# Four matmul banks, longer rings and second expert weights addressed by a register, in the sparse mixture of a two-layer gated network

## The chip, the cores and the metric

One core of one Trainium2 chip runs the whole program. The metric is device time in microseconds (us) of one execution. Engines are TensorE (PE, its weight loads PEld), VectorE (DVE), ScalarE (ACT), GpSimd (POOL) and SyncE (SP, here a queue of DMA issues).

## The reference

Inputs are x (128 x 64 x 128, which is 8192 tokens of 128 numbers) and a context (128 x 64 x 96). Everything is float32.

```python
x = x + tanh(g_xattn[0]) * cross_attention_16_heads(layernorm(x), ctx)      # layer 0
x = x + tanh(g_ffn[0])   * mixture_of_6(layernorm(x))    # all 6 experts, 64 hidden, weights of the best 2
x = x + tanh(g_xattn[1]) * cross_attention_1_head(layernorm(x), ctx)        # layer 1
x = x + tanh(g_ffn[1])   * mixture_of_8(layernorm(x))    # the change is here
# mixture_of_8: logits = x @ Wg; the two largest, softmax over the two; for each expert e
#   h = silu(x @ W1[e]) * (x @ W2[e])        128 -> 256
#   out += (h @ W3[e]) * weight[e]           256 -> 128
```

## The kernel before

The first phase (up to about 320 us) is the 16-head attention, in 64 tiles of 128 tokens. The second phase (function mixtures_and_attention) does the first mixture, the second attention and the routing of the last mixture in 16 groups of 512 tokens, as a software pipeline over STEPS, and then the last mixture as a sparse one. The queues of the engines are written out by hand: each engine has its own unrolled list of calls, and semaphores are the only link between them.

The sparse mixture works on sorted rows. For each token the two chosen experts give two rows, which POOL scatters with indirect DMAs (L1105, 8 for each group) into a table in HBM sorted by expert. The table is worked off in DTILES = 142 tiles of 128 rows (71 for each half of the tokens), each of one expert; a plan made on DVE gives the first row and the expert of every tile. Step t of `sparse(t)`, one for each engine, does:

- SP: the load of the rows of tile t (L1063, ring of 7 buffers).
- PE: the hidden matmuls of tile m = t - HIDDEN (L1741: four logical 128x128x128 float32 matmuls, W1 and W2 of the expert, recorded as 8), the transpose of tile t (L1751, one record), and the output matmuls of tile w = t - OUT (L1760: two logical, recorded as 4). Then it raises `ends_mm`. The hidden matmuls raise `hidden_mm`.
- ACT: silu of tile t - HIDDEN out of the bank (L1510), and a copy of W1 and W2 of tile t's expert, 128x512, from the resident weights into a ring of 3 (L1517).
- DVE: waits for `ends_mm` of t + 1, which is PE's step t; copies the transposed tile to SBUF (L1285), keeps its token numbers and weights (L1286), multiplies silu by the second half of the bank for tile t - HIDDEN (L1290, raises `h_ready`), scales the output of tile t - OUT (L1301, raises `share_ready`), and copies W3 of tile t's expert, 128x256, into a ring of 8 (L1307). Every fourth step it first loads four expert numbers into registers (`four_tiles`, L902).
- POOL: one indirect DMA (L1113) for each tile, which scatters its 128 scaled rows to their tokens' places in a table of contributions. `keep_shares(b)` does four tiles.

With HIDDEN = 2 and OUT = 4 the waits between the steps are these. PE's hidden matmuls of step t wait for `h_ready` m - 1, the product of tile t - 4, which DVE makes in its step t - 2: there are two hidden banks, `uv[m % 2]`. PE's output matmuls of step t wait for the product of tile t - 4 and the share of tile t - 6, both from DVE's step t - 2. DVE's step t waits for PE's step t. ACT's silu waits for `h_ready` m - 1 too (two silu buffers).

The first 17 steps are woven into what is left of groups 14 and 15 of the dense part: in POOL's queue `keep_shares(0)` (tiles 0 to 3) stands before the scatter of group 14, and `keep_shares(1)` and `keep_shares(2)` stand before the scatter of group 15. From step 108 on DVE also adds contributions of the first half to X (L1322). After the last tile the contributions of the second half are loaded (eight loads of 512 KB), added (L1328, L1330) and stored.

## Time and profile before

| | |
|---|---|
| median of 3 runs | 926.17 us (923.63 to 931.97) |
| profiled execution, its own time | 930.39 us |
| span of the profiled execution | 928.6 us, 1.8 us less than its time |
| mean granted TensorE clock | 0.933 |
| PE busy | 793.4 us, 85% |
| DVE, ACT, POOL busy | 720.4, 571.9 and 466.9 us |

Busy time is the time in which an engine had an instruction running. Starts of PE's records are measured and their ends are modelled; starts and ends of DVE and ACT are measured. The number in brackets at the end of a line of the timeline is how long the engine had been idle and who ended that.

### The profile page before, as it was taken

The page shows a single profiled execution, that of the slowest core. Times are in us where ns is not written, and L with a number is a line of the kernel's source. Part 1 is how long each engine was busy: PE and PEld are TensorE (multiplying, and loading weights), DVE is VectorE, ACT ScalarE, POOL GpSimd, SP SyncE. Part 2 cuts the span into 40 slices and gives each one's busy share as a digit, 9 for nine tenths or more (in the row PEclk, how much of TensorE's full clock was granted, in tenths as well). Part 3 has the DMA queues.
Part 4 walks back from the last instruction along what each step waited for, and adds up shares of the span by engine and source line. Part 5 has one row for each costly group of instructions (what it writes and reads, how often), then busy time and mean ns, then how long its engine had stood idle before and what let it go on. Part 6 is the DMA issues. An engine that isn't in the chain of part 4 may idle for free. (4 is left out here: it accounts for less than half of the span.)

```text
span 928.6 us, 26325 instructions
## 1 busy us (share of the span) xinstructions
PE 793.4 (85%) x8408; PEld 610.8 (66%) x8408; DVE 720.4 (78%) x3041; ACT 571.9 (62%) x1209; POOL 466.9 (50%) x504
## 2 busy tenths in 40 slices
PE   4999999999999599999998898865678888888870
PEld 2566666666666356677775676765577887888860
DVE  3989899889898769899999988644465666668864
ACT  3777777777776456887887766443334555555530
POOL 3653454445444011376676765646555554555550
PEclk9999999999999879989999989877779999999995
DMA  9001001000100200011111111311122322245628
GB/s 242 30 23 41 20 20 37 22 20 20 39 1 2 59 1 10 13 50 45 46 45 39 53 44 35 88 49 58 58 67 73 96 79 69 78 125 163 178 81 277
DMA packets 62211, 57.95 MB, mean 62 GB/s; under 512 B 10320, under 2 KB 52099, under 8 KB 62115
## 3 DMA queue, kind: packets, MB, share of 16 engines
q1 hardware_dynamic: 44547, 34.25, 13.2%
q0 software_dynamic: 8640, 17.84, 5.7%
q10 hardware_dynamic: 8928, 4.70, 1.8%
q8 instruction: 45, 0.74, 0.3%
q14 instruction: 51, 0.42, 0.2%
HBM read 32.74 MB, written 24.02 MB: 61 GB/s over the span
## 5 line engine op out<-in xcount | busy, mean ns | idle before, releaser
L1113 POOL DMA_INDIRECT contributions<-v_heads,d_token x142 | 136.6, 962 | 120.4 <-DVE v_heads L1301 76.2
L1741 PE MATMUL bc_bank<-d_xT,d_w 128*128 128x128 f32 x1136 | 161.9, 288 | 39.7 <-DVE b_hidden L1290 17.1
L1741 PEld LDWEIGHTS bc_bank<-d_xT,d_w 128*128 128x128 f32 x1136 | 145.7, 201 | 46.8 <-DVE d_xT L1285 35.1
L1105 POOL DMA_INDIRECT sorted_rows<-r_send,r_slots x128 | 126.8, 990 | 50.2 <-issue 34.6
L1510 ACT ACTIVATE b_hidden<-bc_bank 128x256 f32<-128x256 f32 x142 | 54.4, 383 | 154.4 <-PE bc_bank L1741 121.1
L1285 DVE COPY d_xT<-bc_bank 128x128 f32<-128x128 f32 x142 | 40.8, 287 | 94.3 <-PE bc_bank L1760 66.3
L432 POOL TENSOR_SCALAR a_k_heads<-a_kT,first 128x512 f32<-128x512 f32 x60 | 93.2, 1570 | 0.8 <-ACT a_kT L483 0.8
L1517 ACT COPY d_w<-w 128x512 f32 x142 | 86.9, 612 | 2.2
L507 ACT ACTIVATE a_probs<-a_scores 128x1024 f32<-128x1024 f32 x64 | 65.6, 1025 | 29.4 <-PE a_scores L607 29.3
L350 DVE TENSOR_REDUCE a_neg_max<-a_scores 128x16 f32<-128x1024 f32 x64 | 78.1, 1220 | 6.8 <-PE a_scores L597 5.3
L514 ACT COPY a_probsT<-a_probsT_bank 128x512 f32<-128x512 f32 x128 | 74.7, 584 | 11.7 <-PE a_probsT_bank L624 11.1
L624 PE MATMUL a_probsT_bank<-first,a_probs 128*128 128x128 f32 x512 | 79.7, 278 | 2.2 <-ACT a_probsT L514 0.3
L347 DVE TENSOR_REDUCE a_denom<-a_probs 128x16 f32<-128x1024 f32 x64 | 77.3, 1208 | 1.7 <-issue 1.3
L597 PE MATMUL a_scores<-a_k_heads,a_qT 32*64 32x256 f32 x1024 | 70.8, 391 | 2.8 <-issue 2.7
L624 PEld LDWEIGHTS a_probsT_bank<-first,a_probs 128*128 128x128 f32 x512 | 57.6, 141 | 12.5 <-issue 5.8
L423 POOL TENSOR_TENSOR X<-X,out_bias 128x512 f32 (+1 forms) x16 | 20.3, 1270 | 87.5 <-ACT a_xn L470 84.8
L1751 PE MATMUL bc_bank<-first,d_rows 128*128 128x128 f32 x142 | 40.6, 286 | 20.7 <-DVE d_xT L1285 14.7
L1586 PE MATMUL bc_bank<-b_xnT,w 128*128 128x512 f32 x96 | 52.9, 666 | 0.9 <-DVE b_weighted L1156 0.9
L1637 PE MATMUL bc_bank<-w,b_weighted 128*128 128x128 f32 x384 | 49.7, 289 | 0.0
L1301 DVE TENSOR_SCALAR v_heads<-bc_bank,d_ends 128x128 f32<-128x128 f32 x142 | 48.8, 344 | 0.5 <-issue 0.5
L1637 PEld LDWEIGHTS bc_bank<-w,b_weighted 128*128 128x128 f32 x384 | 46.9, 202 | 1.8 <-issue 0.4
L1760 PE MATMUL bc_bank<-w_in,b_hidden 128*128 128x128 f32 x288 | 46.8, 288 | 0.5 <-issue 0.5
(215 smaller groups left out, 1884.8 us busy)
## 6 DMA issues: line engine op xcount, KB each, us to landing
d_rows<-sorted_rows SPq DMA_DIRECT2D x142, 65.0 KB
X<-in_x SPq DMA_DIRECT2D x16, 256.0 KB, 3.0
b_hidden<-contributions SPq DMA_DIRECT2D x8, 512.0 KB
b_weighted<-contributions SPq DMA_DIRECT2D x8, 512.0 KB
out_x<-X ACTq DMA_DIRECT2D x16, 256.0 KB
ctxT<-in_ctx_T SPq DMA_DIRECT2D x16, 192.0 KB, 2.9
c_ctxT<-in_ctx_T SPq DMA_DIRECT2D x16, 192.0 KB
contributions<-v_heads,d_token POOLq DMA_INDIRECT x142
```

The source lines that it names most:

```text
L347: dve.reduce_sum(denom[:], probs[u % 2][:].rearrange("p (h k) -> p h k", k=S), AX_X).then_inc(sum_done, 1)
L350: dve.tensor_reduce(neg_max[:], scores[u % 2][:].rearrange("p a (h k) -> p (a h) k", k=S), AX_X, ALU.max, negate=True).then_inc(max_done, 1)
L432: last = pool.tensor_scalar(keys_of_head(par, j), kT[:], c.head_of_group[:, j:j + 1], None, ALU.mult)
L507: act.activation(probs[(u + 1) % 2][:], scores[(u + 1) % 2][:].rearrange("p a n -> p (a n)"), ACT.Exp, scale=SCALE0).then_inc(exp_done, 1)
L514: act.copy(probsT[u % 2][:, half * HU // 2:(half + 1) * HU // 2, :].rearrange("p u q -> p (u q)"), probsT_bank[:]).then_inc(pT_ev, 1)
L597: last = pe.matmul(scores[u % 2][S * b:S * b + S, s, bass.ts(h, 4 * S)], qT[par][rows_in, h, tile, :], k_heads[par][rows_in, tile, h].rear ...
L624: last = pe.transpose(probsT_bank[:, bass.ts(k, P)], probs[u % 2][:, bass.ts(half * HU // 2 + k, P)], c.ident[:])
L1105: pool.indirect_dma_start(dispatch.rows, bass.IndirectOffsetOnAxis(ap=slots[n % 2][:, k, j:j + 1], axis=0), send[n % 2][k][:, j, :], None) ...
L1113: pool.indirect_dma_start(dispatch.contributions, bass.IndirectOffsetOnAxis(ap=token[:, t % KEEP:t % KEEP + 1], axis=0), shares[t % KEEP], ...
L1517: act.copy(w12[t % 3][:], c.w12[:, bass.ds(experts[t % 4], 1)].rearrange("d a i h -> d (a i h)")).then_inc(w12_ready, 1)
L1637: last = pe.matmul(y[:, bass.ts(j, P)], weighted[n % 2][:, k, bass.ts(j, P)], c.w2_0[:, k, :], start=(k == 0), stop=(k == C0 - 1))
L1741: last = pe.matmul(uv[m % 2][:, bass.ts(i, P)], w12[m % 3][:, bass.ts(i, P)], xT[m % 4][:], start=True, stop=True)
```

## The change

Four edits, all in the sparse mixture.

1. The hidden matmuls use four banks instead of two from tile 20 (FOUR) on: banks 0 and 1 and the two halves of `pair`. Up to tile 19 they use banks 0 and 1 in turn, because `pair` is still used by groups 14 and 15. PE's wait before them becomes `h_ready` m - 3 from tile 24 on and stays m - 1 up to tile 21; tiles 22 and 23 wait for the last uses of `pair`.
2. The steps lie further apart: HIDDEN is 3 instead of 2, the product on DVE has a distance of its own, GATED = 4, and OUT is 6 instead of 4. So in step t PE does the hidden matmuls of tile t - 3 and the output matmuls of tile t - 6, ACT the silu of tile t - 3, and DVE the product of tile t - 4 and the share of tile t - 6. The whole takes 148 steps of PE and DVE instead of 146.
3. The ring of silu buffers has 4 instead of 2, in space that was there; ACT waits for `h_ready` m - 3.
4. The copy of W3 on DVE is gone, with its semaphore and its register loads. PE reads W3 where it lies, `c.w3[:, bass.ds(experts[w % 4], 1), k]`, as the moving operand at an address from a register. For this PE loads four expert numbers into its registers every fourth step.

```diff
--- before.py
+++ after.py
@@ -975,16 +975,15 @@
     STEPS = range(-1, G + 3)
 
     KH = HID1 // P
-    HIDDEN, OUT = 2, 4
+    HIDDEN, GATED, OUT, FOUR = 3, 4, 6, 20
     KEEP = 32
     ROWS = 7
     rows = [sb(f"d_rows{i}", [P, ROW], F32) for i in range(ROWS)]
     xT = [sb(f"d_xT{i}", [D, P], F32) for i in range(4)]
     w12 = [sb(f"d_w12_{i}", [D, 2 * HID1], F32) for i in range(3)]
-    w3 = [c.w3_in[:].rearrange("p e k d -> p e (k d)")[:, i] for i in range(8)]
     tails = [b[:, C0 - 1, i * KH * P:(i + 1) * KH * P] for b in hidden + weighted for i in range(2)]
-    silu = tails[0:2]
-    d_hidden = [b.rearrange("p (k n) -> p k n", k=KH) for b in tails[2:6]]
+    silu = tails[0:4]
+    d_hidden = [b.rearrange("p (k n) -> p k n", k=KH) for b in tails[4:8]]
     shares = [c.v_heads[i // (KEEP // 2)][:].rearrange("p g u s -> p (g u s)")[:, i % (KEEP // 2) * D:i % (KEEP // 2) * D + D]
               for i in range(KEEP)]
     token = sb("d_token", [P, KEEP], U32)
@@ -992,13 +991,16 @@
     both = [b[:].rearrange("p c n -> p (c n)")[:, 0:GT * 2 * D].rearrange("p (t k d) -> p t k d", t=GT, k=2)
             for b in hidden + weighted]
 
-    uv, y_bank = bank[0:2], (bank[5], bank[2])
+    y_bank = bank[5], bank[2]
+
+    def uv(m):
+        return (bank[0][:], bank[1][:], pair[:, 0], pair[:, 1])[m % 2 if m < FOUR else m % 4]
 
     def tr_bank(t):
         return bank[4] if t > 16 and t % 2 else bank[3]
 
     d_loaded = [sem(f"d_loaded{i}") for i in range(ROWS)]
-    d_xT_ready, row_read, w12_ready, w3_ready = (sem(f"d_{n}") for n in ("xT_ready", "row_read", "w12_ready", "w3_ready"))
+    d_xT_ready, row_read, w12_ready = (sem(f"d_{n}") for n in ("xT_ready", "row_read", "w12_ready"))
     hidden_mm, ends_mm, silu_done, h_ready, share_ready = (sem(f"d_{n}") for n in ("hidden_mm", "ends_mm", "silu_done", "h_ready", "share"))
     kept = [sem(f"d_kept{i}") for i in range(8)]
     pair_loaded = [sem(f"d_pair_loaded{i}") for i in range(4)]
@@ -1273,8 +1275,6 @@
                     wait_alone(dve, dot_step, 2 * n + 2)
                     top.choose(dve, n)
 
-            experts = [None] * 4
-
             def sparse(t):
 
 
@@ -1284,11 +1284,11 @@
                         dve.wait_ge(hidden_mm, t - 3)
                     dve.tensor_copy(xT[t % 4][:], tr_bank(t)[:, 0:P]).then_inc(d_xT_ready, 1)
                     dve.tensor_copy(ends[:, t % KEEP, :], rows[t % ROWS][:, D:ROW]).then_inc(row_read, 1)
-                m = t - HIDDEN
+                m = t - GATED
                 if 0 <= m < DTILES:
                     dve.wait_ge(silu_done, m + 1)
-                    dve.tensor_tensor(d_hidden[m % 4].rearrange("p k n -> p (k n)"), silu[m % 2],
-                                      uv[m % 2][:, KH * P:2 * KH * P], ALU.mult).then_inc(h_ready, 1)
+                    dve.tensor_tensor(d_hidden[m % 4].rearrange("p k n -> p (k n)"), silu[m % 4],
+                                      uv(m)[:, KH * P:2 * KH * P], ALU.mult).then_inc(h_ready, 1)
                 w = t - OUT
                 if w >= 0:
                     dve.wait_ge(row_read, w + 1)
@@ -1300,11 +1300,6 @@
                         dve.tensor_copy(token[:, here], ends[:, here, 0])
                     dve.tensor_scalar(shares[w % KEEP], y_bank[w % 2][:, 0:D], ends[:, w % KEEP, 1:2], None,
                                       ALU.mult).then_inc(share_ready, 1)
-                if t < DTILES:
-                    if t % 4 == 0:
-                        dve.wait_ge(dispatch.planned, 1 if t + 4 <= HALF_TILES else 2)
-                        experts[:] = dispatch.four_tiles(mybir.EngineType.DVE, dispatch.tile_expert, t, E1 - 1)
-                    dve.tensor_copy(w3[t % 8], c.w3[:, bass.ds(experts[t % 4], 1)].rearrange("p a b d -> p (a b d)")).then_inc(w3_ready, 1)
                 g, q = (t - ADDS_AT) // 4, (t - ADDS_AT) % 4
                 if 0 <= g < GH:
                     add_piece(g, q // 2, q % 2)
@@ -1505,9 +1500,9 @@
                 m = t - HIDDEN
                 if m >= 0:
                     act.wait_ge(hidden_mm, m + 1)
-                    if m >= 2:
-                        act.wait_ge(h_ready, m - 1)
-                    act.activation(silu[m % 2], uv[m % 2][:, 0:KH * P], ACT.Silu).then_inc(silu_done, 1)
+                    if m >= 4:
+                        act.wait_ge(h_ready, m - 3)
+                    act.activation(silu[m % 4], uv(m)[:, 0:KH * P], ACT.Silu).then_inc(silu_done, 1)
                 if t < DTILES:
                     if t % 4 == 0:
                         act.wait_ge(dispatch.planned, 1 if t + 4 <= HALF_TILES else 2)
@@ -1726,6 +1721,8 @@
                         last = pe.transpose(pT_bank[:, bass.ts(j, P)], probs[:, j, :], c.ident[:])
                     last.then_inc(pT_mm, 1)
 
+            experts = [None] * 4
+
             def sparse(t):
 
 
@@ -1733,12 +1730,16 @@
                 if 0 <= m < DTILES:
                     pe.wait_ge(d_xT_ready, m + 1)
                     pe.wait_ge(w12_ready, m + 1)
-                    if m >= 2:
-                        pe.wait_ge(h_ready, m - 1)
+                    if m < 2:
+                        pe.wait_ge(k_ready if m == 0 else weighted_ready[0], G)
+                    elif m == FOUR + 2:
+                        pe.wait_ge(xrT_ready, G)
+                    elif m == FOUR + 3:
+                        pe.wait_ge(x1_updated, G)
                     else:
-                        pe.wait_ge(k_ready if m == 0 else weighted_ready[0], G)
+                        pe.wait_ge(h_ready, m - 1 if m < FOUR + 2 else m - 3)
                     for i in range(2 * KH):
-                        last = pe.matmul(uv[m % 2][:, bass.ts(i, P)], w12[m % 3][:, bass.ts(i, P)], xT[m % 4][:], start=True, stop=True)
+                        last = pe.matmul(uv(m)[:, bass.ts(i, P)], w12[m % 3][:, bass.ts(i, P)], xT[m % 4][:], start=True, stop=True)
                     last.then_inc(hidden_mm, 1)
                 if t < DTILES:
                     pe.wait_ge(d_loaded[t % ROWS], 16 * (t // ROWS) + 16)
@@ -1751,13 +1752,16 @@
                     last = pe.transpose(tr_bank(t)[:, 0:P], rows[t % ROWS][:, 0:D], c.ident[:])
                 if w >= 0:
                     pe.wait_ge(h_ready, w + 1)
-                    pe.wait_ge(w3_ready, w + 1)
+                    if w % 4 == 0:
+                        pe.wait_ge(dispatch.planned, 1 if w + 4 <= HALF_TILES else 2)
+                        experts[:] = dispatch.four_tiles(mybir.EngineType.PE, dispatch.tile_expert, w, E1 - 1)
                     if w >= 2:
                         pe.wait_ge(share_ready, w - 1)
                     else:
                         pe.wait_ge(q_ready if w == 0 else chosen_ready, G - w)
                     for k in range(KH):
-                        last = pe.matmul(y_bank[w % 2][:, 0:D], d_hidden[w % 4][:, k, :], w3[w % 8][:, bass.ts(k, D)],
+                        last = pe.matmul(y_bank[w % 2][:, 0:D], d_hidden[w % 4][:, k, :],
+                                         c.w3[:, bass.ds(experts[w % 4], 1), k].rearrange("p a d -> p (a d)"),
                                          start=(k == 0), stop=(k == KH - 1))
                 last.then_inc(ends_mm, 1)
```

## Rows read from the trace of the kernel before

**Rows 1.** Windows, whole stretches; columns are named in its first line.

```profile
core 0: us, PE busy (x) PEld busy (x) DVE busy (x) ACT busy (x) POOL busy (x), PEclk, DMA share, GB/s
692.70:837.60 144.90, 123.89 (x1055) 119.37 (x1054) 93.47 (x431) 73.61 (x162) 77.46 (x81) 1.00 0.30 86
837.60:898.80 61.20, 52.22 (x434) 50.65 (x433) 48.88 (x207) 30.37 (x67) 32.30 (x34) 0.97 0.50 149
898.80:928.60 29.80, 3.53 (x30) 3.18 (x28) 14.04 (x28) 0.84 (x3) 5.75 (x6) 0.63 0.70 236
```

**Rows 2.** Line L1285 from 692.6 us on: DVE's steps.

```profile
L1285 DVE COPY d_xT<-bc_bank x115: 270/291/293, 692.7 to 898.8; 128x128 f32<-128x128 f32 x115
...
  PE bc_bank L1760: 59.6, 55
```

**Rows 3.** Timeline 703 to 710 us, PE and DVE: start, us, engine, line.

```profile
700.81 0.61 PE L1760 MATMUL bc_bank<-w_in,b_hidden 128*128 128x128 f32 x4
...
703.41 0.29 DVE L1285 COPY d_xT<-bc_bank 128x128 f32<-128x128 f32 x1 [2.25 <-PE bc_bank L1760]
...
704.25 1.13 PE L1741 MATMUL bc_bank<-d_xT,d_w 128*128 128x128 f32 x8 [1.38 <-DVE b_weighted L1290]
...
705.32 0.61 PE L1760 MATMUL bc_bank<-w_in,b_weighted 128*128 128x128 f32 x4
...
705.77 1.06 PE L1741 MATMUL bc_bank<-d_xT,d_w 128*128 128x128 f32 x8
705.97 0.29 DVE L1285 COPY d_xT<-bc_bank 128x128 f32<-128x128 f32 x1 [0.28 <-PE bc_bank L1760]
...
706.58 0.35 DVE L1301 TENSOR_SCALAR v_heads<-bc_bank,d_ends 128x128 f32<-128x128 f32 x1
...
706.77 0.61 PE L1760 MATMUL bc_bank<-w_in,b_weighted 128*128 128x128 f32 x4
...
707.22 1.06 PE L1741 MATMUL bc_bank<-d_xT,d_w 128*128 128x128 f32 x8
...
708.74 0.29 DVE L1285 COPY d_xT<-bc_bank 128x128 f32<-128x128 f32 x1 [1.62 <-PE bc_bank L1760]
...
709.02 0.41 DVE L1290 TENSOR_TENSOR b_hidden<-b_hidden,bc_bank 128x256 f32<-128x256 f32 x1
...
709.58 1.13 PE L1741 MATMUL bc_bank<-d_xT,d_w 128*128 128x128 f32 x8 [0.75 <-DVE b_hidden L1290]
```

**Rows 4.** Groups by line, 692 to 838 us.

```profile
L1113 POOL DMA_INDIRECT contributions<-v_heads,d_token x83 | 79.5, 957 | 68.8 <-DVE v_heads L1301 45.0 <-issue 23.8
...
L1510 ACT ACTIVATE b_hidden<-bc_bank 128x256 f32<-128x256 f32 x82 | 31.4, 383 | 71.0 <-PE bc_bank L1741 66.4 <-issue 3.2 <-DVE b_hidden L1290 1.0
...
L1307 DVE COPY w_in<-w 128x256 f32 x82 | 23.7, 289 | 0.0
```

**Rows 5.** Register work of the sequencers, lines L902, L563 and L591.

```profile
L902 ACTq TENSOR_LOAD <-plan_tile_expert x36: 304/309/517, 606.8 to 896.5; - x36
L902 DVEq TENSOR_LOAD <-plan_tile_expert x36: 339/344/598, 608.0 to 897.6; - x36
...
L563 PEldq FUSED_REGOPS  x12: 78/83/91, 55.0 to 257.5; - x12
...
L591 PEldq FUSED_REGOPS  x6: 51/51/52, 54.2 to 238.3; - x6
```

**Rows 6.** Line L1285 up to 692.6 us: the first 27 steps.

```profile
L1285 DVE COPY d_xT<-bc_bank x27: 269/291/292, 608.0 to 691.5; 128x128 f32<-128x128 f32 x27
...
  remote: 20.2, 4
```

**Rows 7.** Timeline 628 to 681 us, POOL.

```profile
636.45 1.00 POOL L1105 DMA_INDIRECT sorted_rows<-r_send,r_slots  x1 [0.30 <-issue]
...
650.58 0.96 POOL L1113 DMA_INDIRECT contributions<-v_heads,d_token  x1 [0.30 <-issue]
655.86 0.96 POOL L1113 DMA_INDIRECT contributions<-v_heads,d_token  x1 [4.32 <-DVE v_heads L1301]
```

## The prediction

> **What bounds the kernel now.** I read the windows first, because the change touches one stage only, and in them the two long stretches from 692.7 to 898.8 us: the sparse mixture by itself. Granted clock is 1.00 and 0.97, and no engine is full: PE is busy for 123.9 of 144.9 us, DVE for 93.5, POOL for 77.5 [rows 1]. The last 29.8 us are DMA (236 GB/s) and adds, and the change doesn't touch them [rows 1]. Then I took the pace from the line that runs once a step, the copy of the transposed tile: 115 steps, first at 692.7 and last at 898.8 us, so 206.1 / 114 = 1.808 us a step [rows 2]. In the first of the two stretches it is 1055 PE records / 13 a step = 81 steps, 1.785 us.
>
> PE alone could go faster. Where it isn't held, one step starts 1.45 us after the last (705.77, 707.22) [rows 3]. So 114 x (1.808 - 1.45) = 41 us of the stage is PE waiting for its partners, and this is all that a better pipeline can give. DVE is busy for 93.5 / 81 = 1.15 us a step [rows 1], and POOL's scatter takes 0.96 plus 0.30 idle = 1.26 us [rows 4, 7]; neither is the bound, but POOL has only 0.19 us of room if PE goes at its own pace.
>
> The timeline shows the loop. PE's step that starts at 704.25 has its last matmul done at 705.32 + 0.61 = 705.93; DVE starts its step at 705.97, 0.04 later. For the next step PE's record ends at 706.77 + 0.61 = 707.38, and DVE starts only at 708.74, though it had been idle for 1.62 us: 1.36 late. Two steps earlier it was 700.81 + 0.61 = 701.42 to 703.41, 1.99 late [rows 3]. DVE waits for nothing but PE's semaphore there; 55 such waits cost it 59.6 us in the stage [rows 2]. So the result of a step becomes visible late when PE has gone on to the next without a break, and at once when PE has just been idle. Ends of PE records are modelled, so I call the difference L, the lateness, and take it as it is; what makes it I can't tell.
>
> **The loop before.** PE's hidden matmuls of step t wait for DVE's step t - 2, which waits for the end of PE's step t - 2. Around two steps: L, then from DVE's copy to the end of its product 709.43 - 708.74 = 0.69, to PE's start 709.58 - 709.43 = 0.15, and PE's whole step 705.93 - 704.25 = 1.68 us [rows 3]. That is 2.52 + L = 2 x 1.79, so L = 1.06 on average, between the 0.04 and 1.99 seen.
>
> **The change, part by part.**
>
> *Four banks and HIDDEN = 3, from tile 24 on.* The hidden matmuls of step t need the product of tile t - 7, from DVE's step t - 3, which is always there. They leave the loop. The silu too has a whole step of slack before DVE's product, and its ring of four doesn't wait; ACT waits for PE alone today (66.4 of its 71.0 idle us in the stretch [rows 4]), so this costs nothing.
>
> *The output matmuls stay in the loop.* The product of tile t - 6 and the share of tile t - 8 both come from DVE's step t - 2, as before. The new loop: L, then DVE's copy to the end of the share, 706.93 - 705.97 = 0.96, then 0.15, then the four output records, 0.61 [rows 3]. That is 1.72 + L for two steps. With L = 1.06 a step is 1.39 us, less than PE's 1.45, with 1.36 it is 1.54 and with 1.99 it is 1.86. What is late next, when the stall before the hidden matmuls goes, is a shorter stall before the output matmuls.
>
> *PE's register work.* The trace has no matmul with a register address and no register load on PE. Nearest rows: four expert numbers load in 0.31 us on ACT and 0.34 on DVE, so 0.08 a tile; an address computation on PE's own sequencer, in the loop of the first phase, is 51 to 83 ns [rows 5]. With one to four such for a tile it is 0.05 to 0.33, together 0.13 to 0.41 us a tile, or nothing if PE's sequencer does it while the array is busy. A gain is excluded, since nothing on PE is removed but a wait for a semaphore that DVE raised steps earlier. I put 0.2 us on the loop of two steps, since the computation stands behind the wait for the share: (1.92 + L) / 2. With L = 1.2, between its average and the 1.36 that a continuing PE shows, 1.56; I take 1.55 us a step.
>
> The register load can be weighed against the Trainium skill. The rows have 0.31 to 0.34 us for a load of four. The Trainium skill (DMA: Bandwidth & Descriptors, latency and other measured facts) gives `tensor_load` a floor of about 600 ns, amortised by unrolling four times; the trace disagrees. By the page it would be 0.15 a tile, 0.07 more, and fully exposed 114 x 0.07 = 8 us more than by the rows.
>
> *The W3 copy leaves DVE.* 82 copies, 23.7 us, mean 289 ns in the first stretch, none of which ended an idle time before it [rows 4]. It stands behind the share, so nothing in the loop waits for it, and DVE isn't full: I cost it at nothing there. Between 837.6 and 898.8 us DVE also adds pieces and is busy for 48.9 of 61.2 us [rows 1]; over 34 steps that is 1.44 us each, near 1.55, and without the copy's 0.29 it is 1.15, so the 1.55 holds in this stretch too.
>
> *Steady stage:* 114 x (1.808 - 1.55) = 29 us less.
>
> *The first 25 steps get worse.* Up to tile 21 the hidden matmuls of tile m wait for the product of tile m - 2, and with GATED = 4 and HIDDEN = 3 that is DVE's step t - 1, not t - 2. PE can't start a step before DVE has answered the last one: 0.04 + 0.69 + 0.15 + 1.68 = 2.56 us a step, with L at its smallest since PE has just been idle. Before, 11 of these steps took less than that, between 1.3 and 2.0 us, in all 11 us less (by the starts of the 27 copies [rows 6]). But this stretch is held by other things: of 84 us for 27 steps, 20.2 are four long waits of DVE for PE [rows 6], and from 636.45 to 651.5 us POOL issues without a break, then idles for 4.32 us until tile 8's share comes [rows 7]. POOL's first three `keep_shares` need DVE's steps 9, 13 and 17 instead of 7, 11 and 15, and the scatter of group 15 stands behind the third. Two steps are 3 to 5 us. Part of both falls into POOL's 4.3 us of idle time, or shortens the long waits. I take 8 us of 0 to 16.
>
> *The end:* two more steps to drain, with only four PE records each; under 2 us, and part of POOL's last scatters hide it. Nothing.
>
> **Sum.** 930.4 - 29 + 8 = 909 us on the profiled execution, whose own time is 4.2 us above the median of the runs shown. On the median: 926.2 - 21 = 905 us.
>
> **The rivals.**
>
> *PE at its own pace.* If L doesn't grow and the register work is hidden, the loop is 1.39 and PE's 1.45 us decides, say 1.47: 114 x 0.338 = 38.5 us, and with nothing lost at the start 888 us. For it: L averages 1.06. Against: only 0.19 us of room for POOL. Chance 0.15.
>
> *L grows.* PE now goes on without a break, and L was largest just when it did. With L = 1.85 the step is 1.79 to 1.89 and all that is left is the worse start: 926 + 8 = 934 us; with L = 1.5 it is 1.71, 11 us gained, 923. One form of this: PE's results come late while POOL issues its scatters back to back. All four long waits, of 20.2 us in all [rows 6], fall into or around POOL's unbroken stretches [rows 7], and at a faster pace POOL has less idle time. The Trainium skill (SBUF — State Buffer, who interferes with whom) says that PE never waits for another engine's port and that DMA never contends with a compute engine. It would exclude this form; the waits stand in the trace all the same. Chance of 917 to 935 us: 0.19.
>
> *Slower: the register work isn't hidden on PE.* The engine with the least room gets instructions that DVE had room for. If a matmul with a register address adds c to PE's own 1.45 us, the stage gives nothing back from the point where 114 x (1.808 - 1.45 - c) equals the 8 us of the start, c = 0.29 us a tile; the upper bound of the rows is 0.41. With c = 0.41 a step is 1.86: 114 x 0.05 = 6 us more, plus 8, is 940 us. For it: PE's sequencer has 26 records and three waits to issue in 1.45 us. Against: the registers of four tiles are loaded once, and right after a wait of 1.38 us PE's eight records take the same 1.13 us as after others [rows 3], so the sequencer keeps up with the array. Chance 0.16, with all that ends over 935.
>
> *The change doesn't do what it says:* if four banks weren't reached in time (tile 23 waits for group 15's last add to X), the wait would lie before 692.7 us; in DVE's queue that add stands before its step 6, and PE's wait at its step 26, so it can't be. Less than 0.01.
>
> **How the numbers follow.** Forecast, 893 to 917 us: 0.50. PE's pace, below 893: 0.15. L grows: 0.19. Slower: 0.16. A measurement of this kernel tells about 1% (9 us) from no change. So faster by over 1% (under 917) has 0.50 + 0.15 = 0.65, within 1% 0.19, slower 0.16. The range leaves out the deep end of the first rival (under 889) and most of the last (over 935).
>
> **What the profile after would show.** The copy L1285 at steps of 1.55 us from step 27 on, in place of groups of three with a gap. PE's idle time, if any, before the output matmuls and with DVE's share as releaser, none before the hidden ones. The distance from PE's modelled end to DVE's start at 1.2 us on average: this is the number that would make me wrong, and if it is above 1.7 the gain is gone. Four output records more than 0.61 us apart in all, or register rows on PE in front of them that end an idle time, would be the last rival. In the first 25 steps a steady idle time of PE of about 1.1 us a step, with DVE's product as releaser. POOL's idle before its scatters down from 68.8 us in 146.

## The result, and the profile after

The changed kernel takes 943.2 us (median of four runs, 932.1 to 948.4), the kernel before 929.1 us (four runs, three of them those of its own section). The ratio leaves out the run of 948.4 us, which counts as slow, and is 1.0126, 95% interval 1.007 to 1.0182. The change makes the kernel slower by 1.3%; the forecast was 905 us. Its profiled execution has a span of 938.6 us, 10.0 more than before.

DVE's copy of the transposed tile, line L1285, comes once a step and splits the 10 us. Its occurrences, the first 24 and the other 118, in the changed kernel:

```profile
L1285 DVE COPY d_xT<-bc_bank x24: 283/292/293, 607.3 to 699.4; 128x128 f32<-128x128 f32 x24
...
  PE bc_bank L1763: 24.9, 11
  remote: 18.4, 4
...
L1285 DVE COPY d_xT<-bc_bank x118: 267/291/293, 703.4 to 905.4; 128x128 f32<-128x128 f32 x118
...
  PE bc_bank L1763: 71.0, 63
...
  PE bc_bank L1752: 9.2, 9
```

And the same two stretches of the kernel before:

```profile
L1285 DVE COPY d_xT<-bc_bank x24: 272/291/292, 608.0 to 686.3; 128x128 f32<-128x128 f32 x24
...
L1285 DVE COPY d_xT<-bc_bank x118: 269/291/293, 688.0 to 898.8; 128x128 f32<-128x128 f32 x118
```

- Steps 0 to 24: 703.4 - 607.3 = 96.1 us, before 688.0 - 608.0 = 80.0. **16 us lost** (the first step came 0.7 us sooner).
- Steps 24 to 141: 202.0 us or 1.726 a step, before 210.8 or 1.802. **9 us gained.**
- From the last copy to the end: 938.6 - 905.4 = 33.2 us, before 29.8. **3.4 us lost.**

A second pair of traces, before_again and change_again in the table below, gives 16.4 lost, 2.7 gained and 3.0 lost. The loss at the start and at the end comes again; the gain between them is 3 to 9 us.

The windows of the changed kernel in these three stretches (columns as in [rows 1]):

```profile
607.00:703.40 96.40, 58.71 (x325) 54.02 (x325) 30.61 (x161) 29.55 (x65) 42.30 (x48) 0.68 0.16 46
703.40:905.40 202.00, 184.82 (x1524) 174.77 (x1524) 123.08 (x537) 102.91 (x235) 111.10 (x116) 0.99 0.38 108
905.40:938.60 33.20, 6.07 (x48) 5.32 (x46) 15.45 (x32) 1.45 (x4) 7.65 (x8) 0.62 0.63 213
```

In the second, PE is now busy for 185 of 202 us: 1.58 us a step, though 13 records 0.111 us apart are 1.45. So of the 32 us that the 117 steps take beyond 117 x 1.45, 15 lie where PE counts as busy and its records are further apart, and 17 are idle. PE's waits in this stretch (us, times, longest) account for all of the idle time but 0.4 us, and none of them stands before the hidden matmuls (L1742), where they all stood before:

```profile
PE bc_bank L1752 <- DVE d_xT L1285: 9.2, 9, 2.7
...
PE bc_bank L1763 <- DVE v_heads L1301: 7.6, 16, 0.6
```

In the same 117 steps of the kernel before PE is idle for 30.0 us, 28.9 of them waiting for DVE's product. The first stretch of the changed kernel has a granted clock of 0.68.

**The start.** PE's timeline from 692 to 703 us, where the clock is at its lower level (granted 0.50, 1.2 GHz, over 691.4 to 703.4 us):

```profile
696.28 2.05 PE L1742 MATMUL bc_bank<-d_xT,d_w 128*128 128x128 f32 x8 [0.87 <-DVE b_weighted L1290]
698.12 0.42 PE L1752 MATMUL bc_bank<-first,d_rows 128*128 128x128 f32 x1
698.33 1.06 PE L1763 MATMUL bc_bank<-w,b_weighted 128*128 x4
700.26 2.04 PE L1742 MATMUL bc_bank<-d_xT,d_w 128*128 128x128 f32 x8 [0.87 <-DVE b_weighted L1290]
```

Each step waits for DVE's product of the step before it: 700.26 - 696.28 = 3.98 us a step. Seven of the 24 steps go so (654.2 to 670.1 and 691.5 to 703.4 us); at 670.1 to 677.8 us, where the granted clock is 0.95, three steps take 2.56 us each, the figure of the prediction. Among the first 24 steps of the kernel before, by the starts of their copies, there is no such series.

**The lateness.** By this I mean the time from the modelled end of the last output matmul of a step on PE to the start of DVE's copy for that step. DVE from 746 to 752 us, and below it PE. The step that ends at 746.63 + 0.61 = 747.24 us on PE is answered at 749.98, 2.74 us late; then DVE does its next two steps at once. PE had gone on at its own pace until 749.59 and then stood still, waiting for DVE:

```profile
746.83 0.34 DVE L1301 TENSOR_SCALAR v_heads<-bc_bank,d_ends 128x128 f32<-128x128 f32 x1
749.98 0.29 DVE L1285 COPY d_xT<-bc_bank 128x128 f32<-128x128 f32 x1 [2.80 <-PE bc_bank L1763]
...
750.91 0.28 DVE L1285 COPY d_xT<-bc_bank 128x128 f32<-128x128 f32 x1
...
751.99 0.29 DVE L1285 COPY d_xT<-bc_bank 128x128 f32<-128x128 f32 x1
```

```profile
746.63 0.61 PE L1763 MATMUL bc_bank<-w,b_weighted 128*128 x4
...
748.53 1.06 PE L1742 MATMUL bc_bank<-d_xT,d_w 128*128 128x128 f32 x8
750.41 0.30 PE L1752 MATMUL bc_bank<-first,d_rows 128*128 128x128 f32 x1 [0.83 <-DVE d_xT L1285]
```

Averaged over steps 24 to 141 it is 1.15 us in the changed kernel and 0.87 in the kernel before.

### The profile page after: what moved, and what is told of

Read it like the earlier page. It is cut to its first block and busy times, and to the rows that moved or that the text cites. A ratio compares the mean times of both kernels' runs of the same rounds, so it can differ in the third digit from the quotient of the medians.

```text
span 938.6 us, 26325 instructions
## 1 busy us (share of the span) xinstructions
PE 806.9 (86%) x8408; PEld 618.1 (66%) x8408; DVE 691.3 (74%) x2899; ACT 568.9 (61%) x1209; POOL 466.1 (50%) x504
## 5 line engine op out<-in xcount | busy, mean ns | idle before, releaser
L1285 DVE COPY d_xT<-bc_bank 128x128 f32<-128x128 f32 x142 | 41.0, 289 | 135.0 <-PE bc_bank L1763 96.0
L1742 PE MATMUL bc_bank<-d_xT,d_w 128*128 128x128 f32 x656 | 100.3, 302 | 35.5 <-DVE b_weighted L1290 28.9
L1742 PEld LDWEIGHTS bc_bank<-d_xT,d_w 128*128 128x128 f32 x656 | 90.7, 214 | 39.4 <-DVE d_xT L1285 37.3
L1763 PE MATMUL bc_bank<-w,b_weighted 128*128 x568 | 96.5, 295 | 9.3 <-DVE v_heads L1301 9.2
L1763 PEld LDWEIGHTS bc_bank<-w,b_weighted 128*128 128x128 f32 x568 | 78.9, 201 | 17.4 <-issue 14.3
L1505 ACT ACTIVATE b_hidden<-bc_bank 128x256 f32<-128x256 f32 x82 | 31.5, 385 | 96.2 <-PE bc_bank L1742 50.7
L1505 ACT ACTIVATE b_hidden<-bc_pair 128x256 f32<-128x256 f32 x60 | 23.0, 384 | 70.5 <-PE bc_bank L1742 40.4
L1742 PE MATMUL bc_pair<-d_xT,d_w 128*128 128x128 f32 x480 | 64.3, 277 | 0.0
L1742 PEld LDWEIGHTS bc_pair<-d_xT,d_w 128*128 128x128 f32 x480 | 59.3, 194 | 0.0
```

What stands on the lines that cost most here:

```text
L1742: last = pe.matmul(uv(m)[:, bass.ts(i, P)], w12[m % 3][:, bass.ts(i, P)], xT[m % 4][:], start=True, stop=True)
L1763: last = pe.matmul(y_bank[w % 2][:, 0:D], d_hidden[w % 4][:, k, :], c.w3[:, bass.ds(experts[w % 4], 1), k].rearrange("p a d -> p (a d)"), ...
```

## The experiments

Each group of runs had a chip of its own, with its own runs of the kernel before, so every ratio is to that chip's. The kernel before took 856 to 947 us on them, a wider spread than any effect of the change, and that became part of the question. All of it in one table (steps from the starts of the copy of the transposed tile, as above; "per step" is over steps 24 to 141, "tail" from the last copy to the end; times in us). Runs with "plain_shares" in their name and one_load_hidden compute something else than the reference; they are there for their times only.

```
run                     before on    ratio, 95% interval       steps 0-24  per step  tail
                        that chip
(kernel before, shown above)                                     80.0      1.802     29.8
(changed kernel)         929.1    1.0126  1.007  to 1.0182        96.1      1.726     33.2
w3_alone                 947.2    1.0067  1.0036 to 1.0098        79.7      1.939     32.4
banks_alone              947.2    1.0124  1.009  to 1.0157        98.2      1.857     34.0
equal_gates              947.2    0.9854  0.9808 to 0.9901        79.1      1.731     32.9
old_gates_banks          947.2    0.9861  0.9805 to 0.9916        77.9      1.756     30.7
before_again             927.6    (one run, 928.9 us)             77.0      1.782     30.0
plain_shares             927.6    0.9565  0.9454 to 0.9675        75.4      1.450     28.9
one_load_hidden          927.6    0.9944  0.9927 to 0.996         85.0      1.663     34.5
before_plain_shares      858.3    0.9946  0.9912 to 0.9979        47.6      1.451     26.6
equal_gates_w3_copy      858.3    1.0009  0.998  to 1.0038        48.3      1.445     32.8
change_again             928.4    1.0091  1.0058 to 1.0124        93.4      1.759     33.0
equal_gates_again        928.4    0.996   0.9916 to 1.0004        77.8      1.764     30.9
w3_copy_again            928.4    1.0072  1.0038 to 1.0106        77.6      1.811     31.5
four_steps_deep          857.1    1.0012  0.9984 to 1.004         47.3      1.448     34.0
four_steps_deep_again    855.9    1.0013  0.9984 to 1.0043        47.9      1.448     33.8
four_steps_deep_third    945.9    0.9874  0.9813 to 0.9935        76.9      1.734     32.7
```

### Parts and distances

**w3_alone**: the kernel before, with

```
-  w3_ready, the ring w3[0..7] and DVE's copy (L1303 to L1307 of the kernel before)
-  pe.wait_ge(w3_ready, w + 1)
+  if w % 4 == 0: pe waits for the plan and loads four expert numbers
-  ... w3[w % 8][:, bass.ts(k, D)]
+  ... c.w3[:, bass.ds(experts[w % 4], 1), k]
```

> The kernel before with one part of the change: the second expert weights read in place by TensorE through a register address, DVE's W3 copy gone; two banks, rings and distances as before. Theory R (the register work costs PE time where PE has none to give): 138 tiles at 0.05 to 0.15 us make it 7 to 20 us slower than the kernel before, and the copy of the transposed tile goes at 1.85 to 1.95 us a step in place of 1.80. Theory N (it is hidden, and DVE's copy hid too): within 4 us of the kernel before, 1.79 to 1.82 us a step.

**banks_alone**: the changed kernel with that edit undone.

> The changed kernel with the second expert weights copied by DVE again, as before: four banks, HIDDEN 3, GATED 4, OUT 6 stay. Theory R: the register work was what ate the gain, so this one is 7 to 20 us faster than the changed kernel and at 1.60 to 1.68 us a step. Theory N: within 4 us of the changed kernel, 12 us slower than the kernel before, at 1.71 to 1.74 us a step, and the first 24 steps are as long as in the changed kernel.

**equal_gates**:

```
-    HIDDEN, GATED, OUT, FOUR = 3, 4, 6, 20
+    HIDDEN, GATED, OUT, FOUR = 3, 3, 5, 20
```

> The changed kernel with GATED 3 in place of 4 and OUT 5 in place of 6, HIDDEN 3 as it is: DVE's product of a tile no longer comes one step after the hidden matmuls' step, so the two-bank stretch needs DVE's step t-2 again and not t-1. Theory S (the chain PE, DVE, PE with one step between, in the first 24 steps, costs the 16 us): step 24 is reached 12 to 16 us sooner than in the changed kernel, the later steps stay at 1.72 to 1.75 us, and the whole is 12 to 16 us faster than the changed kernel, 0 to 5 us faster than the kernel before. Rival (the start is held by POOL's late shares and the row loads, not by the chain): step 24 comes less than 6 us sooner.

**old_gates_banks**: banks_alone with `HIDDEN, GATED, OUT, FOUR = 2, 2, 4, 20`.

> The kernel before with the four banks alone: HIDDEN 2, GATED 2, OUT 4, W3 copied by DVE, but banks and silu ring of four from tile 20 on. Theory S: the first 24 steps as in the kernel before within 3 us. The later steps tell whether the larger distances bring anything: if the hidden matmuls' wait for their bank was the loop, 1.72 to 1.75 us a step, 6 to 9 us faster than the kernel before; if the loop goes through the output matmuls, which still need DVE's step t-2, and the silu of the step that has just ended, 1.77 to 1.80 us a step and no difference.

Theory S holds: with GATED equal to HIDDEN the first 24 steps take 79.1 us (77.8 in the repeat) where the changed kernel has 96.1 (93.4) and banks_alone 98.2, and the whole is faster than the changed kernel by 12 us on one chip (0.996 against 1.0091 of 928 us) and 25 us by the ratios of two (0.9854 against 1.0126). The rival, that the start is held by the shares that come later on POOL, isn't needed. Here OUT went from 6 to 5 together with GATED, but four_steps_deep_third (below) has OUT 6 again with GATED 3, is the same kernel up to step 24 otherwise, and takes 76.9 us on a chip with late results. And the series of 3.98 us a step is gone. In the first 24 steps of equal_gates DVE's waits for PE by name have shrunk, 24.9 to 7.5 us; those labelled "remote", explained below, have not (18.4 to 25.6):

```profile
L1285 DVE COPY d_xT<-bc_bank x24: 272/290/292, 609.6 to 687.2; 128x128 f32<-128x128 f32 x24
...
  remote: 25.6, 4
  PE bc_bank L1763: 7.5, 9
```

old_gates_banks is as good as equal_gates: 1.756 us a step, 13 us faster than the kernel before, more than the 6 to 9 expected of it. So what gains on this chip is the four banks; the greater distance of the hidden matmuls, with W3 in place, adds nothing to the whole (0.9854 beside 0.9861). The distance alone, with all else equal, was not run on one chip.

Theory R fell. W3 in place cost 0.7% with two banks (6 us, just under the 7 expected), and its 1.939 us a step lies in the theory's range, though the kernel before has no trace on that chip to compare with. But in that run PE waits before its hidden matmuls alone, 46 us for DVE's product, and never before the output matmuls, where the register work stands. Undone in the changed kernel it gave nothing back by the ratios on two chips (1.0124 beside 1.0126), at 1.857 us a step, a pace that neither theory had. And at equal gates, side by side on one chip, in place was better by 1.1% (equal_gates_again, w3_copy_again, below). No price of register work on PE comes out; its four-number loads take 0.33 us each. Where nothing is late, the pace is the same with W3 in place (1.450 in plain_shares, 1.448 in four_steps_deep) and copied (1.451 in before_plain_shares, 1.445 in equal_gates_w3_copy).

### What makes PE's results late

**before_again** is the kernel before.

> The kernel before once more, for a profile on the same chip as the next ones: 1.79 to 1.90 us a step after step 24, 80 us for the first 24 steps. No theory differs here; it is the measure for the other three.

It has 1.782 us a step and 77.0 us for the first 24 steps, both a little under that.

**pe_alone_and_scatters** holds only this on PE, with no wait (in short):

```
for t in range(30):
    4 x pe.matmul(bank[t % 2][:, 128 i : 128 i + 128], w_i, xT)   -> increments hid
    pe.transpose(...)
    2 x pe.matmul(bank[3 + t % 2], ...)                           -> increments end
POOL: 39 x pool.indirect_dma_start(table, slots[:, i], src)       (stretches b, d, f)
SP:   39 x sp.dma_start(table rows, src)                          (stretch c)
```

> A kernel of its own that computes nothing of the reference (its output is x): six stretches of 30 steps, each with PE's work of one step and no wait on PE, four hidden matmuls on four loads, one transpose, two output matmuls. a: PE alone; b: with POOL's indirect scatters back to back; c: with the same bytes as plain transfers; d: the hidden matmuls as one load with 512 columns, with scatters; e: with copies on DVE and ACT; f: e with scatters. Small copies on DVE and ACT after each step tell when its result is really there. Theory T1 (PE's true pace for load and matmul in turn is slower than its records of 1.45 us a step): DVE's copies come 1.65 to 1.75 us apart in a, b, c, e and f alike, and under 1.45 in d. Theory T2 (POOL's descriptor work holds PE's results back): 1.45 in a, c and e, and in b and f over 1.65 or copies late by 1 to 3 us in groups. Theory T3 (the transfers themselves hold them back): c is like b. Theory T4 (none of these; the lateness is of the loop's own copies): 1.45 everywhere, and no lateness.

Alone, PE keeps 1.45 us a step and DVE's small copy comes 1.45 us after the last; with 39 plain transfers (c) too. Windows of a, b and c:

```profile
24.00:65.00 41.00, 41.00 (x366) 41.00 (x366) 4.75 (x28) 5.36 (x28) 0.00 (x0) 1.00 0.01 1
72.00:119.00 47.00, 17.29 (x105) 14.93 (x104) 1.41 (x6) 0.96 (x5) 35.73 (x38) 0.65 0.15 53
158.00:199.00 41.00, 41.00 (x370) 41.00 (x370) 4.74 (x28) 5.39 (x28) 0.00 (x0) 1.00 0.22 64
```

105 PE records in 47 us beside POOL's scatters, 370 in 41 us beside the plain transfers, which move more (64 against 53 GB/s). T2 holds, T1 and T3 fall. The other stretches agree: with scatters DVE's copies fall behind in the same way when the hidden matmuls are one load with 512 columns (d, up to 18 us apart) and with copies on DVE and ACT (f, 20 us), and with those copies and no scatters (e) they come 1.45 us apart. DVE in stretch b: the results come at distances that double, to 25 us:

```profile
73.70 0.34 DVE L38 COPY tiny<-xT 128x2 f32<-128x2 f32 x1 [1.28 <-PE bank L31]
75.45 0.17 DVE L38 COPY tiny<-xT 128x2 f32<-128x2 f32 x1 [1.42 <-PE bank L31]
79.07 0.17 DVE L38 COPY tiny<-xT 128x2 f32<-128x2 f32 x1 [3.45 <-PE bank L31]
86.14 0.17 DVE L38 COPY tiny<-xT 128x2 f32<-128x2 f32 x1 [6.90 <-remote]
100.19 0.40 DVE L38 COPY tiny<-xT 128x2 f32<-128x2 f32 x1 [13.89 <-remote]
125.42 0.58 DVE L38 COPY tiny<-xT 128x2 f32<-128x2 f32 x3 [24.82 <-remote]
```

And PE, which waits for nothing in this kernel, starts single matmuls 2.80 us apart. Its idle time is labelled "issue", for which the profile has no releaser:

```profile
113.41 0.37 PE L31 MATMUL bank<-w 128*128 128x128 f32 x1 [2.43 <-issue]
116.21 0.37 PE L31 MATMUL bank<-w 128*128 128x128 f32 x1 [2.43 <-issue]
```

So a late result isn't only a late message: PE itself is stopped. But it is late before PE is stopped. The scatters begin at 70.43 us, and PE keeps its own pace until 80.0:

```profile
77.33 0.61 PE L31 MATMUL bank<-w 128*128 128x128 f32 x4
...
78.78 0.61 PE L31 MATMUL bank<-w 128*128 128x128 f32 x4
```

The records of these two steps end at 77.94 and 79.39; DVE's copies for them come at 86.14 and 100.19, 8 and 21 us later. So the results get stuck first, and PE's own records slow down some 5 us after the first late copy (75.45). Whether PE stops because its results can't get out, or both have a cause of their own, no run shows. "Remote" in DVE's waits stands here for a result of PE that came so late that the profile matched no instruction to it; the four long waits of [rows 6] carry the same label.

**plain_shares**: the changed kernel, and in **before_plain_shares** the kernel before, with this (abridged)

```
-  pool.indirect_dma_start(contributions, token[:, t % KEEP], shares[t % KEEP])     (142 of them, L1113)
+  sp.dma_start(contributions[bass.ts(t, P), :], shares[t % KEEP])
```

> The changed kernel with POOL's 138 indirect scatters of the shares replaced by as many plain transfers of the same 64 KB on SP's queue, to rows in the order of the tiles; what is added to X later is so not each token's own share, the work is the same. T2: with POOL's descriptor work gone PE's results are no longer late and a step after step 24 falls from 1.67 to 1.80 to under 1.58 us, 12 to 25 us less than the changed kernel. T1: 1.65 to 1.80 us a step as before, within 5 us of the changed kernel, and the lateness stays.

> The kernel before (two banks, old distances, W3 copied by DVE) with POOL's indirect scatters of the shares replaced by plain transfers on SP's queue, as in plain_shares; rows in the order of the tiles, so the sums are others. Theory P (POOL's scatters alone hold both kernels above PE's own pace): 1.45 to 1.50 us a step after step 24, 885 to 892 us where plain_shares has 886, so four banks bring nothing once POOL is silent. Theory Q (with PE prompt the two banks are the next limit): 1.55 to 1.65 us a step, 12 to 24 us more than plain_shares.

plain_shares goes at 1.450 us a step, PE's own pace, with PE busy for the whole of the stretch:

```profile
681.60:851.40 169.80, 169.80 (x1525) 169.80 (x1525) 125.65 (x537) 107.69 (x235) 0.00 (x0) 1.00 0.48 129
```

The bytes are the same and the DMA share higher (0.48); what is gone are POOL's indirect scatters. With them goes the lateness: 0.04 us on average over these steps, where the changed kernel has 1.15. The whole is 52 us less than the changed kernel (0.9565 against 1.0126 of 928 us, on two chips), more than the 12 to 25 expected. Against before_again on the same chip the 117 steps save 117 x (1.782 - 1.450) = 39 us. Theory P holds in that before_plain_shares has 1.451 with two banks and the old distances, but its chip has no lateness (below), so how the old rings would do on a late chip without scatters was not seen.

**one_load_hidden**: the changed kernel with (abridged)

```
-  for i in range(2 * KH): pe.matmul(uv(m)[:, 128 i ...], w12[m % 3][:, 128 i ...], xT[m % 4])
+  pe.matmul(uv(m), xT[m % 4], w12[m % 3])
```

> The changed kernel with the hidden matmuls of a tile as one load of the transposed rows and 512 columns of weights streamed over it, in place of four loads with 128 columns each; the blocks come out transposed, so the values are others, the columns streamed by PE, the bytes and all other instructions are the same. T1: the loads are what makes PE slower than its records, so the pace after step 24 falls to 1.35 to 1.60 us a step, 15 to 35 us less than the changed kernel. T2: PE's pace was not what held the step, so 1.65 to 1.80 us a step remain after step 24.

1.663 us a step: T1's pace (1.35 to 1.60) doesn't come, T2's does. The whole is 17 us less than the changed kernel, by the ratios on two chips (0.9944 and 1.0126), which lies in T1's 15 to 35; half of it or more is in the first 24 steps (85.0 us, 8 to 11 less). So the loads aren't what makes PE late, but fewer PE instructions cost less here; how much of that is the chips' difference isn't known.

### Which transfers, and on which chip

**equal_gates_w3_copy** is equal_gates with DVE's W3 copy. **what_holds_pe** is a second probe with ten stretches.

> The run equal_gates (HIDDEN 3, GATED 3, OUT 5, four banks) with the second expert weights copied by DVE again. If reading them in place costs PE time, as the 6 us of w3_alone suggest, it is 4 to 8 us faster than equal_gates, a ratio of 0.976 to 0.982 to the kernel before; if reading in place helps at this faster pace, since DVE's step is shorter, it is 2 to 6 us slower, 0.988 to 0.992; if it makes no difference, 0.983 to 0.988.

> A kernel of its own (its output is x), ten stretches with 24 steps of PE's work of one step and small copies on DVE and ACT after each; a: 30 indirect scatters of 128 rows back to back on POOL, as in the run before; b: one scatter a step, when the step's result is there; c: 64 rows each; d: indirect gathers; e: plain transfers issued by POOL; f: copies on POOL, no DMA; g: a as before, but PE waits for DVE's answer each step; h: a, with bf16 matmuls; i: a, with one semaphore increment a step; j: a, with PE idle and DVE and ACT answering each other. If POOL's writing of descriptors holds up PE's own stream: a stalls with gaps that double, c less, d and perhaps e like a, f not at all, b goes at 1.6 to 1.8 us a step, i like a, and j shows DVE and ACT prompt. If instead semaphores of all engines are held up: j stalls too, and i less than a. If it is POOL at work of any kind: f stalls like a. If PE is held only when it never pauses: g stays prompt.

Neither showed any lateness to speak of (0.08 us on average in equal_gates_w3_copy), and the kernel before took only 858 us on this chip. Nothing in the theories had foreseen that, and the prices expected of the W3 copy could not be read here. The probe on it goes at 1.45 us a step under the same unbroken scatters (0.96 + 0.30 us). So the three runs on this chip (before_plain_shares is the third) settle nothing about cause, but one thing about size. Against before_again (77.0 us for the first 24 steps, 1.782 a step), equal_gates_w3_copy has 48.3 us and 1.445: 28.7 + 117 x 0.337 = 68 us, which is the 69 us between the kernel before on the two chips. **The lateness is worth some 70 us.** With it gone the kernel before must be near PE's own pace too: it has no trace on such a chip, but equal_gates_w3_copy takes the same time there (1.0009).

The same probe and three versions on a further chip, where the kernel before takes 928 us:

> The probe of ten stretches once more, unchanged; it computes nothing of the reference. On a chip where the kernel before takes over 900 us: a stalls with gaps that grow, f (copies on POOL, no DMA) goes at 1.45 us a step, e (plain transfers issued by POOL) at 1.45 if it is the indirect descriptors and stalls if it is any descriptor written by POOL; h (bf16, a third of PE's time a step) stalls less if PE's fp32 load and matmul pairs are what is held up; j is prompt if it is PE alone. On a chip where the kernel before takes 860 us: all stretches at 1.45 as in the last call.

> The changed kernel once more. On a chip with late results (before over 900 us): 1.01 to 1.02 times the kernel before. On a chip without (before near 860 us): PE's own pace, 1.45 us a step in both, so the steady stage gives nothing; the start costs what the chain of one step costs at full clock, 2.56 less 2.0 us for 22 steps, and the drain 1 to 3 us, so 1.01 to 1.02 there too.

> The run equal_gates once more. On a chip with late results: 0.98 to 0.99 times the kernel before, 20 to 28 us less than the changed kernel. On a chip without: 0.998 to 1.004, since nothing but the drain differs from the kernel before, and 8 to 15 us less than the changed kernel.

> The run equal_gates_w3_copy once more, beside equal_gates itself on one chip. If TensorE reading through a register address costs nothing: within 4 us of equal_gates_again. If it costs PE 0.05 us a tile: 5 to 9 us faster than that. On a chip with late results the kernel has not been seen; 0.98 to 0.99 times the kernel before is expected by the same reasons.

Windows of the probe, each while POOL works: a (scatters of 128 rows), b (one scatter a step), c (64 rows), d (gathers), e (plain transfers issued by POOL), f (copies on POOL), g (PE waits for an answer each step), h (bf16), i (one increment a step), j (PE idle):

```profile
25.80:63.50 37.70, 17.19 (x112) 15.69 (x111) 1.19 (x7) 1.15 (x6) 28.87 (x30) 0.66 0.15 51
93.60:125.20 31.60, 31.39 (x282) 31.20 (x280) 4.17 (x22) 4.23 (x22) 20.13 (x21) 1.00 0.13 43
134.80:170.70 35.90, 13.31 (x90) 11.89 (x88) 0.95 (x5) 0.77 (x4) 26.99 (x30) 0.67 0.11 27
204.80:242.00 37.20, 16.33 (x105) 14.07 (x104) 1.15 (x6) 1.15 (x6) 28.36 (x30) 0.69 0.18 52
273.80:289.90 16.10, 16.10 (x146) 16.10 (x146) 2.12 (x12) 2.11 (x11) 16.02 (x30) 1.00 0.34 115
309.50:331.70 22.20, 22.20 (x201) 22.20 (x201) 5.07 (x16) 2.88 (x15) 18.44 (x30) 1.00 0.01 2
346.00:383.70 37.70, 12.12 (x78) 10.77 (x78) 1.09 (x6) 0.96 (x5) 28.87 (x30) 0.72 0.15 51
425.00:462.60 37.60, 11.38 (x101) 7.38 (x98) 1.90 (x10) 2.09 (x11) 28.77 (x30) 0.62 0.15 51
476.90:514.50 37.60, 17.30 (x105) 14.64 (x103) 1.02 (x6) 1.15 (x6) 28.77 (x30) 0.65 0.15 51
542.30:554.60 12.30, 0.00 (x0) 0.00 (x0) 4.43 (x20) 4.04 (x21) 9.56 (x10) 0.53 0.14 48
```

Stretch a of the probe on the chip without lateness, for comparison:

```profile
26.00:58.00 32.00, 31.88 (x286) 31.68 (x285) 4.22 (x23) 4.23 (x22) 24.37 (x26) 1.00 0.15 51
```

Scatters and gathers both stop PE, with 64 rows as with 128, in fp32 and bf16, with one increment as with two. Plain transfers issued by POOL don't, at twice the bytes a second (e, 115 GB/s beside 51), nor does POOL's own work, and DVE and ACT answering each other (j: 20 and 21 copies in 12.3 us, 21 and 21 on the other chip) are not held up. So it is indirect DMA on POOL against PE, on this chip. g refutes that a PE that pauses is safe. b, one scatter a step, in groups of at most five 1.26 us apart and with pauses of up to 1.6 us between the groups, costs almost nothing (282 records in 31.6 us, 0.112 us each), though DVE's copies in it are up to 3.6 us apart: in this probe it takes scatters that come close upon each other, and many of them, to stop PE. In the mixture, as I read it (no run shows this step alone), a late share lets the next scatters queue up, and they then go out 1.26 us apart. Such series are no longer than five there after step 24 either, and the changed kernel loses 0.28 us a step all the same: why short series cost so much more in the mixture than in b stays open.

The changed kernel gives 1.0091 here, as expected. equal_gates gives 0.996, a smaller gain than 0.9854 and outside the 0.98 to 0.99 expected, and now 1.0 is just inside its interval. It is 12 us faster than the changed kernel by the ratios, not 20 to 28; its first 24 steps keep the 15.6 us, but the steady pace, 1.764, is no better than the changed kernel's 1.759. Beside it the W3 copy costs 1.1%, at 1.811 us a step, which none of its expectations had.

### Deeper rings

**four_steps_deep**, three times; equal_gates with

```
-    HIDDEN, GATED, OUT, FOUR = 3, 3, 5, 20
+    HIDDEN, GATED, OUT, FOUR, SHARED = 3, 3, 6, 20, 24
+    from step 24: bank[3], bank[4], bank[5], bank[2] in turn hold the transposed rows (columns 0:128)
+    and the output (128:256) of one step (in short; the waits below from step 26 on)
-    pe.wait_ge(d_xT_ready, t - 1), pe.wait_ge(share_ready, w - 1)
+    pe.wait_ge(share_ready, w - 3)
```

> The run equal_gates with OUT 6 in place of 5 and, from step 24 on, one bank for both the transposed rows (columns 0 to 127) and the output of a step (128 to 255), four such banks in turn, beside the four of the hidden units: PE then needs DVE's step t-3 for the product and t-4 for the banks, not t-2. On a chip with late results (before over 900 us). Theory loop (lateness costs only what exceeds the slack of the rings, now 3 x 1.45 less 1.7 = 2.6 us): 1.46 to 1.60 us a step after step 24, 15 to 30 us faster than the kernel before, 0.965 to 0.985. Theory stop (PE itself is stopped while POOL scatters): 1.70 to 1.80 us a step and 0.99 to 1.01, like equal_gates. On a chip without late results: 1.45 us a step and 1.00 to 1.005.

> The run four_steps_deep once more. On a chip with late results (before over 900 us), theory loop: 1.46 to 1.60 us a step after step 24 and 0.965 to 0.985 times the kernel before; theory stop: 1.70 to 1.80 us a step and 0.99 to 1.01. On a chip without: 1.00 to 1.005 as in the last call.

> The run four_steps_deep a third time. On a chip with late results (before over 900 us), theory loop: 1.46 to 1.60 us a step after step 24 and 0.965 to 0.985 times the kernel before; theory stop: 1.70 to 1.80 us a step and 0.99 to 1.01. On a chip without: 1.00 to 1.005, as twice before.

Two chips had no lateness and could tell nothing; on the third, with the kernel before at 946 us, 1.734 us a step, where equal_gates has 1.731 with rings of two steps (on a chip with 947 us), and 0.9874 beside 0.9854. The pace is in the range of theory stop; the ratio lies between the two theories' ranges. I had built this version on the loop theory, and the loop theory falls: a DVE answer may now be three to four steps old and nothing is gained. The lateness is 2.24 us on average there, twice that of equal_gates (1.13), at the same pace. Of the 33 us that PE takes beyond its own pace, 13 are waits for DVE's copy (L1290); the other 20 are idle time that the profile calls "issue" or lie where PE counts as busy. DVE's steps from 24 on, in the third run, still wait as long for PE:

```profile
L1290 DVE COPY d_xT<-bc_bank x118: 267/291/296, 685.5 to 888.4; 128x128 f32<-128x128 f32 x118
...
  PE bc_bank L1773: 66.5, 48
  remote: 13.6, 4
```

## Why the prediction was wrong, point by point

**What bounds the kernel** was read rightly as to place (1.45 us is PE's own pace, POOL has little room) and wrongly as to kind: all 41 us were called PE waiting for its partners, "all that a better pipeline can give". By [rows 1] PE is busy for 123.9 + 52.2 = 176.1 of the 206.1 us, so only 30 are waits; the other 11 us lay where PE counts as busy. plain_shares shows that the 41 us exist (39 us), four_steps_deep_third that a better pipeline doesn't give them.

**Steady stage, forecast 29 us, measured 9 (3 in the second pair).** This is the step that failed, and what failed in it is the formula (1.92 + L) / 2, a loop of two steps in which L is a delay of fixed size, and not the value of L. L was put at 1.2 after the change, and the trace has 1.15. With that the formula gives 1.54 us a step; 1.726 was measured. It didn't describe the kernel before either: L there was computed back from the pace (1.06), and never averaged over the steps; with the 0.87 of the trace the loop gives 1.70 in place of 1.80. The sign that the prediction named for being wrong, L above 1.7, did not come, and the gain was gone all the same.

What the runs showed in its place: the longer rings did take away waits of PE for DVE, as forecast, from 28.9 us to 16.8 and, with four steps, 13.1. The pace followed for 9 us at most and then no further (the three traces are of chips at 929, 929 and 946 us), since PE lost time with nobody to wait for, 12, 16 and 20 us in the same three kernels, and the lateness rose from 0.87 to 1.15 and 2.24. With POOL's scatters of the shares gone all of it is gone (1.450 us a step). L is not a delay that a ring can hide: results of PE get out late while POOL scatters, and PE itself is stopped. A queue with too slow an outlet would look like this, longer with every buffer and no faster; that it is one is a guess.

The rival "L grows" had 0.19, and its named form, PE's results late while POOL scatters back to back, is what the probes confirmed; its size is not, since L grew by 0.3 and not to 1.5 or 1.85, and its 917 to 935 us missed too.

**The first 25 steps, forecast 8 us of 0 to 16, measured 16.** The mechanism was right and was shown (equal_gates, and four_steps_deep_third with OUT 6); the term was mis-sized. The chain was priced at full clock, 2.56 us. Seven steps ran at 3.98 with a granted clock of 0.50, 7 x 1.42 = 10 us, about what is missing. [Rows 1] already had a stretch at 0.63 where PE idles; a chain that idles PE for 0.87 us a step had to be priced at both clocks.

**The end, forecast 0, measured 3.4 us.** Two more steps of drain: the last output matmul ends 7.6 us after the last copy (913.0 us), before 4.0 (902.8), and of this 1.5 us is a wait for DVE's share. That is as much as the whole difference in this pair. On chips with late results, and with the scatters, five runs with OUT 6 have 32.7 to 34.5 us, three with OUT 5 30.9 to 32.9, four with OUT 4 29.8 to 32.4. The groups overlap, so a part may be the spread; "POOL's last scatters hide it" was at least not the whole.

**PE's register work** (0.13 to 0.41 us a tile) and **the W3 copy at nothing**: neither shows as a cost of its own. The prediction's sign for register work, four output records more than 0.61 us apart, is half there: in the changed kernel 63 of the 117 groups of four take 0.61 to 0.63 us, and 53 take 0.67 to 0.74; before it was 116 at 0.61. But banks_alone and w3_copy_again, with W3 copied and no register address on PE, have 33 and 39 such groups, and plain_shares and four_steps_deep, with the register address, none. So the longer groups are not the register's; all but one of them are in runs with late results. The runs that change W3's place alone differ by -1.1 to +0.7% with the setting they are put in. The rival "register work isn't hidden" ended on the right side for a reason that isn't there.

**The sum:** -9 + 16 + 3 = +10 us, in place of -29 + 8. The range to 935 was left because three terms went wrong to the same side. The Trainium skill (SBUF — State Buffer, who interferes with whom), which would have excluded POOL holding up PE, was weighed with the waits in the trace against it; the probe's 105 records in 47 us disagree with it where indirect DMAs are issued, and the 370 in 41 us agree for plain transfers.

## What to carry to other kernels

When a consumer sees results later than the producer's records end, don't compute the delay back from the pace and put it into a pipeline formula. Average it over all the steps, see how much of the producer's lost time is idle at all, and measure the pair alone, with each other engine's work beside it, before rings are made deeper. A ring that is made longer later in the loop needs its distances (here GATED and HIDDEN) equal as long as the ring is short, or the short stretch turns into a chain of one step, and that chain idles PE, so it has to be priced at the lower clock too. And compare on one chip: the kernel before spanned 856 to 947 us from chip to chip.

## What the hardware showed that I had not expected

- Indirect DMAs that POOL issues 1.26 us apart stop PE on some chips: from 0.111 us between the starts of matmuls to 2.80 us, and PE's results reach DVE 3.6, 7.1, 14 and 25 us apart. It builds up: for the first 9.6 us of such a series PE kept its own pace, and groups of up to five scatters cost the probe almost nothing. Plain transfers of the same size, from SP or POOL, don't stop it. Three of the seven groups' chips (the kernel before at 856 to 858 us) show nothing of it in kernels with the same scatters, and the number that results give for the chip was once the same for one of 947 and one of 858 us. Whether it is the chip, its neighbours or its state at the time stays open, and so does which part POOL and PE share.
- Where it exists it is worth some 70 us of 928 in this kernel, more than any change to the rings: 29 in the first 24 steps and 39 after them. Every execution on record has a span and a granted clock, as a traced one has; none shows whether it is the same in an execution that isn't traced.
- W3's copy on DVE goes with slightly longer scatters on POOL: on one chip 0.993 us on average with it (w3_copy_again) and 0.958 without (equal_gates_again). On chips without the lateness it is 1.017 with it (equal_gates_w3_copy) and 1.004 without (four_steps_deep), so there most of the difference to 0.958 is not the copy's. All of it, with the 0.30 us between scatters, still fits under 1.45.
- The best version that was run is equal_gates: 0.985 and 0.996 times the kernel before on two chips with late results. On a chip without, it ran only with the W3 copy, at 1.001; the changed kernel was not run on such a chip.
